# The last layer of a gated three-layer network: its second half's first block made ahead of the first half's first block, and the last block split one block later

## The reference

```
h = silu(_tlin(x, w1_w, w1_s)) * _tlin(x, w2_w, w2_s)
h = gelu(_tlin(h, h1_w, h1_s))
h = gelu(_tlin(h, h2_w, h2_s))
ffn = _tlin(h, w3_w, w3_s)
...
g = _silu(ffn)
x = x + s * g
```

## Time and profile before

| what | value |
|---|---|
| median of 3 runs | 1257.03 us |
| the profiled execution, its span | 1258.56 us, 1256.8 us |
| PE busy | 1245.0 us, 99% of the span |
| DVE busy | 1023.1 us, 81% |
| ACT busy | 925.2 us, 74% |
| POOL busy | 277.1 us, 22% |
| granted TensorE clock, mean | 0.999 |

### The profile page before, as it was taken

The page is one execution under the profiler, slowest core; times in us unless marked ns, Lnnn a source line. Parts: engine busy times, 40 slices in busy tenths (PEclk is TensorE's granted clock), DMA queues, the critical chain, the costliest instruction groups (busy, mean ns, idle before and its releaser), DMA issues.

```text
span 1256.8 us, 16576 instructions
## 1 busy us (share of the span) xinstructions
PE 1245.0 (99%) x5982; PEld 821.0 (65%) x5982; DVE 1023.1 (81%) x1406; ACT 925.2 (74%) x1405; POOL 277.1 (22%) x325
## 2 busy tenths in 40 slices
PE   8999999999999999999999999999999999999997
PEld 6665676666766666666666666666676666766666
DVE  7979879877898778977889778888788877887675
ACT  4556667788677796777877778777787777787664
POOL 7964322020221102211022110311104030040000
PEclk9999999999999999999999999999999999999999
DMA  9589942575225752257413574145731466323431
GB/s 353 222 334 287 330 171 84 174 228 167 110 96 167 221 184 79 101 187 228 164 68 128 182 231 138 68 143 185 233 118 68 165 189 216 109 84 135 148 137 36
DMA packets 97351, 209.48 MB, mean 167 GB/s; under 512 B 13424, under 2 KB 16624, under 8 KB 96240
## 3 DMA queue, kind: packets, MB, share of 16 engines
q1 hardware_dynamic: 80032, 156.98, 36.7%
q0 software_dynamic: 17232, 51.39, 13.4%
HBM read 175.78 MB, written 38.83 MB: 171 GB/s over the span
## 4 chain that ended last, share of the span: by engine, by line
PE 96%; DVE 2%; DMA 1%; ACT 1%; issue 0%; SPq 0%
PE ps L971 62%; PE ps L899 11%; PE ps L1030 9%; PE ps L827 6%; PE ps L926 4%; DMA quad<-in_win 1%; PE ps L1006 0%; PE ps L1003 0%; PE ps L995 0%; PE ps L992 0%; PE ps L987 0%; PE ps L984 0%; PE ps L999 0%; DVE split_lo L1637 0%; DMA xin<-in_x 0%
## 5 line engine op out<-in xcount | busy, mean ns | idle before, releaser
L971 PE MATMUL ps<-split_hi,ring 128*128 128x512 f32 x1792 | 453.5, 404 | 1.4 <-ACT split_hi L1188 1.4
L971 PE MATMUL ps<-split_lo,ring 128*128 128x512 f16 x1792 | 406.3, 380 | 0.0
L971 PEld LDWEIGHTS ps<-split_hi,ring 128*128 128x128 f32 x1792 | 336.8, 188 | 83.8 <-ACT split_hi L1188 1.9
L1637 DVE SCALAR_TENSOR_TENSOR split_lo<-quad,split_hi 128x1024 f16<-128x1024 f32 x224 | 278.9, 1253 | 131.0 <-ACT split_hi L1188 130.4
L971 PEld LDWEIGHTS ps<-split_lo,ring 128*128 128x128 bf16 x1792 | 166.5, 98 | 214.2 <-issue 29.4
L1188 ACT ACTIVATE split_hi<-quad 128x1024 fp32r<-128x1024 f32 x224 | 231.6, 1048 | 33.7 <-PE ps L971 32.0
L1232 ACT ACTIVATE quad<-quad,cols_s 128x512 f32<-128x512 f32 x192 | 136.3, 719 | 51.8 <-DVE quad L1670 29.5
L1662 DVE TENSOR_TENSOR quad<-quad 128x1024 f32<-128x1024 f32 x128 | 157.2, 1261 | 0.0
L650 POOL TENSOR_TENSOR quad<-quad,s 128x256 f32<-128x256 f32 x56 | 52.0, 957 | 382.6 <-ACT quad L1224 382.6
L634 POOL DMA_DIRECT2D z_h<-xin x56 | 55.7, 1001 | 99.6 <-DVE xin L1498 99.6
L684 POOL DMA_DIRECT2D seen<-in_h x32 | 17.6, 551 | 250.0 <-ACT signs L1269 250.0
(11 more groups left out here) (206 smaller groups left out, 1821.5 us busy)
## 6 DMA issues: line engine op xcount, KB each, us to landing
ring<-hs SPq DMA_DIRECT2D x428, 256.0 KB, 3.7
xin<-in_x SPq DMA_DIRECT2D x16, 512.0 KB, 4.1
s_h<-s SPq DMA_DIRECT2D x16, 512.0 KB, 2.6
seen<-in_h POOLq DMA_DIRECT2D x32, 256.0 KB, 3.9
res<-in_x SPq DMA_DIRECT2D x15, 512.0 KB, 5.5
out<-res SPq DMA_DIRECT2D x15, 512.0 KB, 3.1
z_h<-xin POOLq DMA_DIRECT2D x56, 128.0 KB, 4.0
xT_hi<-z_h POOLq DMA_DIRECT2D x14, 512.0 KB, 6.3
```

What stands on the lines that cost most here:

```text
L971: mm = e.matmul(ps[:, 4 * (w % 2) + m, :], weights, moving, start=first and k == 0 and begins, stop=last and k == Q - 1 and not begins, sk ...
L1637: e.scalar_tensor_tensor(out=both(slots_lo[i], g), in0=both(quad[at[t][L][FAST[w][1]]], g), scalar=POWER[L], in1=both(slots_hi[i], g).bitc ...
```

## The change

In all tiles but the last, `down` takes b22 first and b11 second (before: b11, then b22). The order of the last tile, `ORDER_END`, which begins with b22 already, stays. Since b21 reuses b11's buffer, its split on ACT and DVE (`high_last`, `low_last` of "b21") moves behind the second block of `down`, and waits for it. The buffers themselves stay as they were.

```
-        ORDER = [("b11", 0, 0), ("b22", 1, 1), ("b12", 1, 0), ("b21", 0, 1)]
+        ORDER = [("b22", 1, 1), ("b11", 0, 0), ("b12", 1, 0), ("b21", 0, 1)]
         ORDER_END = [("b22", 1, 1), ("b12", 1, 0), ("b11", 0, 0), ("b21", 0, 1)]
...
-            return use[name] if name != "b21" else use[order_of(t)[0][0]]
+            return use[name] if name != "b21" else use["b11" if t < END else "b22"]
...
                 elif name == "b21":
-                    on.wait_ge(down_mm, n_down(t, 0, NB - 1))
+                    on.wait_ge(down_mm, n_down(t, place_of(t, "b11") if t < END else 0, NB - 1))
...
-                    if n == 0:
+                    if n == (1 if t < END else 0):
                         for g in range(2):
                             high_last(t, "b21", g)
...
-                    if n == 0:
+                    if n == (1 if t < END else 0):
                         for g in range(2):
                             low_last(t, "b21", g)
```

## The result

The changed kernel takes 1273.78 us (median of 4 runs, 1273.51 to 1274.44), the kernel before 1257.06 us (its 4 runs beside it): 1.3% slower, ratio 1.0132 (95% interval 1.0119 to 1.0145), or 16.7 us. The forecast was 1272.4 us with a range of 1265.5 to 1277.

The account below looks back on a forecast made before the run. PE was taken to bound the kernel, busy 99% with no waits in the middle tiles. First pause 8.96 plus second 6.4 gave 15.4 us on the profiled 1258.56, 1273.9, less 1.5 for the median: 1272.4 us, range 1265.5 to 1277.

Parts of the forecast that it names:

- the rival by which something else paces the 448 matmuls: Square layers: something other than PE, say weights by DMA, sets their pace; loss made good, 1257.0 us; chance 3%.
- First pause: Start of `down`, tiles 0 to 6: PE waits for piece 2's gelu; 1.23 us each, 1.58 in tile 0, sum 8.96.
- The 0.15 us from gelu to matmul: Start of `down`: time from the end of piece 2's gelu to PE's first matmul, 0.15 us.
- Second pause: Gate stage: matmuls n = 2 wait for ACT's L1140, delayed behind b21's split; 0.91 us a tile, 6.4 us.
- E: The end of the second block of `down`; 322.80 in tile 1 before the change.
- the later b21 itself would be in time: `down`: b21's parts are there by E + 2.1 and E + 3.5, with the third block's 3.6 us lying between.
- only the first pause comes: Rival: DVE and ACT catch up before the gate stage's n = 2; 1266.0 us; chance 12%.
- a delay that goes on: Rival, behind the two L1140 in the gate stage: 0.6 us more lost a tile, to 1276.6 us; chance 11%.
- The rival of a costlier table: ACT's table load after a late silu: 1.28 us more a tile, 9.0 in all, to 1281.4 us; chance 1%.
- the 1282.1: The costlier table's time in the prediction's list of cases, 1282.1 us; chance 1%.
- The correction of 1.5 us: Whole kernel: median of runs, 1257.03, is 1.5 us below the profiled execution, 1258.56; turns 1273.9 into 1272.4 us.

Follow-up runs that it names:

- the move of `rows_high`: Second `rows_high` moved from ahead of piece 2's gelu to behind piece 3's, tiles 0 to 6: changed kernel 1267.44 us, kernel before 1257.3 us.
- the added work: Two extra ACT activations of 384 columns ahead of piece 2's gelu, tiles 0 to 6: changed kernel 1281.11 us, kernel before 1257.13 us.
- the row sums' move: Changed kernel with the row sums' high and low parts moved ahead of b21's split: 1267.2 us, ratio 1.0078 to the kernel before.
- the late split alone: Kernel before, b11 still first, only b21's split moved behind the second block and waiting for it: 1264.28 us, ratio 1.0053.

## Why the prediction was right, point by point

**What bounds the kernel.** PE does, in every stage of a tile. Each pause put in came out at the end at full size, and the stages behind it took none of it back: from tile 1's first L1030 (315.32) to tile 2's first L971 (369.90) it is 54.58 us, against 53.51 before (312.69 to 366.20), and those 1.07 us more are the second pause and 0.08 us. Nor do the square layers run faster behind a pause: from tile 1's first L971 to its last eight it is 98.12 us (213.94 to 312.06), against 98.13 before (212.53 to 310.66). A tile takes 155.96, where 155.8 was forecast. That rules out the rival by which something else paces the 448 matmuls. One reading of the prediction is a little too wide: PE has all its matmuls ready in tiles 1 to 6, but in tile 0 it waits once for 1.4 us, in its square layers at 108.89. It lies ahead of `down` and changes nothing in the sum.

**First pause.** 1.23 forecast and 1.23 measured in tile 1, 1.58 and 1.57 in tile 0. The 0.15 us from gelu to matmul, read in the last tile, held in the others. Shown by the move of `rows_high` and by the added work.

**Second pause.** 0.91 us a tile forecast, 0.98 measured. The steps on ACT and DVE behind E came nearly as worked out. F_lo starts at E + 1.29, not E + 1.18, since DVE begins 1.19 us behind ACT's start of a high part, as the earlier trace rows have it for L1168 and L1631; L1751 comes at E + 8.64 where E + 8.58 was forecast. These 0.06 us don't reach PE: the second L1140 ends at 339.86 and the pair's second matmul starts at 339.92, 0.06 behind it and not 0.15. So that matmul is 0.88 late (339.92 less 336.05, against 336.34 less 333.35), and two small errors nearly cancel. The step behind it is what makes 0.98 of it: 0.33 us (to 340.25), where it was 0.23.

```profile
339.92 0.50 PE L899 MATMUL ps<-split_hi,w 128*128 128x512 f32 x1
```

That the later b21 itself would be in time was right, with more room than the prediction counts: the third block takes 5.4 us (325.79 to 331.19), since matmuls of `seven` stand in it, and not 3.6. Shown by the row sums' move and by the late split alone. The rival "only the first pause comes" falls with it, and so does the one of a delay that goes on: behind the second pause ACT soon waits for PE again (0.60 us before the second pair of L1144), and `mix` and the square layers begin no later than the two pauses make them.

**The table.** The silu now ends at 336.52 and L1220 starts at 337.83, 1.31 us behind it, as before, though the silu is now on the path that PE waits for. The rival of a costlier table falls. (Its 1281.4 us follow from the rows, 1257.03 + 15.4 + 9.0; the 1282.1 in the prediction's list of cases takes the 9.7 us instead, which rest on the page alone.) The extra drain that the Trainium skill gives (ScalarE: Activation LUTs, What ACT_TABLE_LOAD costs) isn't seen here either.

**What the sum lacked**, 15.4 where 16.7 was measured. The term left out is the longer step of PE behind a pause. From the first matmul to the ninth of `down` it was 0.95 us before (313.64 less 312.69) and is now 1.03 (316.35 less 315.32). It stood in the rows already: alone, the first L1030 is 0.36 long in the last tile, where PE had waited, and 0.28 in tile 1. That is 0.08 x 7 = 0.6 us. The second pause's 0.07 more a tile (0.08 in tile 0) is another 0.5, which gives the 16.4 counted in the tiles; the last 0.3 of the 16.7 isn't located. All are small, but the sum of a forecast that rests on seven equal tiles takes each seven times. The correction of 1.5 us from the profiled execution to the median was right: by it the 16.4 us counted in the tiles and 1257.0 give 1273.4.

## What to carry to other kernels

Where the bound engine has no waits at all, ask of a reordering only when each of its operands and banks comes free, and by whose queue: a block put first in a stage takes over the wait for the last result of the stage before, with all that stands ahead of that result on its engine. A step that is moved later is often in time for its own reader and late for those behind it: follow the queue behind it, on each engine, to the next wait of the bound engine, and compare the delay with the slack there. Here a delay of 1.3 us met a slack of 0.32 and cost 7 us in all; a delay below the slack would, by the same reckoning, have cost nothing.

## What the runs showed that was not expected

The pauses of PE cost more than their length: the first matmul of `down` behind one takes 0.08 us longer to the next one's start (the row is 0.36 long in place of 0.28), after a pause of 0.27 us as after one of 1.23, and with the late split alone, where PE doesn't wait there, the first eight take 0.95 us as before. In `down` the wait always comes together with b22 as the first block, so that these rows alone don't tell the two apart. A wait elsewhere does: in the kernel before, with the order unchanged, the L971 behind tile 0's wait is 0.50 long, and others of its kind 0.39; the L899 at 339.92 above is 0.50 long, too.

```profile
108.89 0.50 PE L971 MATMUL ps<-split_hi,ring 128*128 128x512 f32 x1 [1.44 <-ACT split_hi L1188]
```

The start of the program differs between executions. The first L971 starts at 57.10 in the profiled execution of the kernel before and at 55.59 in that of the changed one, and in those of the seven experiments at 55.5 to 56.9, though nothing was changed there:

```profile
57.10 0.58 PE L971 MATMUL ps<-split_hi,ring 128*128 128x512 f32 x1
```
```profile
55.59 1.72 PE L971 MATMUL ps<-split_hi,ring 128*128 128x512 f32 x6
```

That is most of why the two spans differ by 15.2 us only, where the medians differ by 16.7. What makes the start early or late wasn't looked into.
